# A four-layer graph kernel on one core: the first aggregation moves ahead of the heads, the head projections and the next graph's openings move behind them, and x rotates through three buffers

## The reference

```
x = LN(x + softmax((x Wq' + bq) (x Wk')' / sqrt(128)) (x Wv' + bv))        # attention over all nodes, mask of ones
x = LN(x + leaky(0.01, ((adj / rowsum(adj)) x) W1' + b1))                  # first aggregation
x = LN(x + heads(x, adj))        # 4 heads: e = leaky(0.2, si + sj), masked by adj, softmax over i, times Wh
x = LN(x + (D^-1/2 (adj + I) D^-1/2 x) B)                                  # second aggregation, D from adj + I
```

## Time and profile before

| | |
|---|---|
| Median of 3 timed executions | 977.44 us (975.45 to 979.87) |
| The profiled execution | 977.33 us, of which the span of instructions is 975.5 us |
| Granted TensorE clock, mean | 0.957 of full speed |
| Busy share of the span: PE, DVE, ACT, POOL | 87%, 75%, 60%, 33% |
| Period of a full step (first score groups at 202.70 and 317.25) | 114.5 us |

### The profile page before, as it was taken

How to read it: one execution, slowest core, us unless ns; L and a number is a source line. 1 busy time by engine, 2 the same in 40 slices (tenths; PEclk the granted TensorE clock), 3 DMA queues, 4 the chain that set the end, 5 groups by cost and what they waited for, 6 DMA issues and landing times.

```text
span 975.5 us, 25298 instructions
## 1 busy us (share of the span) xinstructions
PE 848.5 (87%) x10856; PEld 683.6 (70%) x10856; DVE 731.0 (75%) x1635; ACT 587.1 (60%) x668; POOL 326.3 (33%) x335
## 2 busy tenths in 40 slices
PE   4988999798998989889998989989899899974874
PEld 2664699556985679746896569856697468962873
DVE  3438777788768787689777887687877798765965
ACT  1564675667665766656846666657665667545513
POOL 2022511633034520626007240355207161064404
PEclk8998999999999999999999999999999999996897
DMA  9823116911178123760268211781237601700260
GB/s 184 123 65 70 41 46 89 164 54 44 50 105 153 45 87 53 121 134 2 87 90 151 66 44 46 97 164 46 76 59 130 111 20 67 89 2 23 67 89 22
DMA packets 166463, 77.39 MB, mean 79 GB/s; under 512 B 136624, under 2 KB 154160, under 8 KB 166352
## 3 DMA queue, kind: packets, MB, share of 16 engines
q1 hardware_dynamic: 156864, 58.48, 31.5%
q0 software_dynamic: 8448, 16.78, 9.7%
q10 hardware_dynamic: 1040, 0.52, 0.2%
HBM read 54.66 MB, written 4.33 MB: 60 GB/s over the span
## 4 chain that ended last, share of the span: by engine, by line
PE 36%; issue 25%; DVE 22%; POOL 7%; ACT 7%; DVEq 0%; POOLq 0%; ACTq 0%
PE ring L1200 7%; PE Z L1222 7%; PE ring L1254 5%; PE Z L1271 4%; DVE x L846 4%; DVE cmat L810 4%; DVE ring L755 3%; PE ring L1235 2%; ACT steps L654 2%; POOL rstd L471 2%; ACT maskb L591 2%; PE ring L1198 2%; DVE meanvar L839 2%; PE ring L1165 1%; DVE x L830 1%
## 5 line engine op out<-in xcount | busy, mean ns | idle before, releaser
L654 ACT ACTIVATE steps<-sjrow,steepsi 128x1024 bf16<-128x1024 f32 x248 | 267.5, 1139 | 123.3 <-DVE cmat L810 94.9
L810 DVE TENSOR_TENSOR cmat<-steps,adj 128x1024 f16<-128x1024 bf16 x180 | 153.6, 896 | 24.6 <-ACT steps L654 22.6
L1254 PE MATMUL ring<-vparts,cmat 128*128 128x66 bf16 x4416 | 146.2, 195 | 16.9 <-DVE cmat L810 12.1
L1222 PEld LDWEIGHTS Z<-vv,probs 128*128 128x128 f32 x1024 | 122.6, 191 | 52.6 <-ACT probs L661 37.3
L1254 PEld LDWEIGHTS ring<-vparts,cmat 128*128 128x128 f16 x4416 | 143.5, 98 | 18.4 <-issue 7.4
L1222 PE MATMUL Z<-vv,probs 128*128 128x129 f32 x1024 | 126.5, 277 | 25.4 <-ACT probs L661 25.4
L1200 PE MATMUL ring<-qT,xT 128*128 128x512 f32 x256 | 139.4, 627 | 0.0
L526 POOL TENSOR_TENSOR cmat<-cmat,ident 128x1024 f16<-128x1024 f16 x8 | 17.1, 2144 | 254.1 <-DMA cmat<-adj 254.1
L755 DVE CUSTOM_DVE_ANT_0 ring<-ring,maskb 128x1024 f32<-128x1024 f32 x64 | 78.3, 1227 | 29.0 <-PE ring L1138 16.3
L661 ACT ACTIVATE probs<-ring 128x1024 f32<-128x1024 f32 x64 | 65.0, 1015 | 52.1 <-PE ring L1200 52.1
L1235 PE MATMUL ring<-vparts,adj 128*128 128x132 bf16 x1536 | 94.0, 222 | 0.0
(11 more groups left out here) (126 smaller groups left out, 1376.3 us busy)
## 6 DMA issues: line engine op xcount, KB each, us to landing
adj<-in_adj_dram POOLq DMA_DIRECT2D x16, 1024.0 KB, 13.0
sjrow<-sj_rows SPq DMA_DIRECT2D x31, 512.0 KB, 4.1
out_dram<-x SPq DMA_DIRECT2D x16, 256.0 KB, 2.4
x<-in_x_dram SPq DMA_DIRECT2D x7, 512.0 KB, 4.3
adjT<-adj SPq DMA_TRANSPOSE x64, 3.5
cmat<-adj SPq DMA_TRANSPOSE x64, 4.5
x<-in_x_dram ACTq DMA_DIRECT2D x1, 512.0 KB, 4.4
small<-in_a_dram SPq DMA_DIRECT2D x1, 128.0 KB, 11.0
```

The source lines that it names most:

```text
L654: act.activation(steps[:, n % STEPS, :], sjrow[:, h % 2, :], ACT.Relu, bias=steepsi[:, t, h:h + 1], scale=STEEP).then_inc(step_made, 1)
L810: dve.tensor_tensor(c_of[:, t, :], steps[:, n % STEPS, :], adjs[o.parity][:, t, :], ALU.min)\
L1222: last = pe.matmul(zq[:, q, 0:D + 1], probs[:, n % 2, j, q * P:(q + 1) * P], vv[:, kt, :], start=kt == 0 and q % 2 == 0, stop=kt == T - 1, ...
L1254: last = pe.matmul(s[:, jt, 0:VW], c_of[:, t, jt * P:(jt + 1) * P], vparts[:, t, h, part, :], start=t == 0 and part == 0, stop=t == T - 1 ...
```

## The change

The list `ORDER` per kind of step becomes one list `SEQ` over all steps, made by `groups_of`. In a full step the first aggregation runs directly behind the mask sums and ahead of head 0, `out1` behind head 0, then heads 1 to 3. Behind head 3 stand the head projections of graph n (`x2T`, `wh`, `sj`) and, between them, the next graph's `xT`, `q` and `v`; then the second aggregation, and `s0` of the next graph between `out3` 0 and 1. The next step begins with `s1`. So the head projections of a graph move from the step after it into its own step, in the first step too, and the last step has none.

With it: `wide` has only four tiles in place of eight and each is used twice in an aggregation; both transposed adjacencies go through the one `adjT`; x rotates through three buffers, in place; `sj` goes through two of the `steps` buffers; ACT makes 14 in place of 17 comparison tiles between the exponentials (`PACE`) and `spread_largest` comes after the second score group; POOL's roots for layer 2 and the degrees come ahead of the diagonal, and the last step fetches all four `sj` rows by DMA.

```diff
+        masks, c = [("mask", 0), ("mask", 1)], [("c", h) for h in range(H)]
+        if n < NB:
+            seq += of(n - 1, *masks, c[0])
+        else:
+            seq += of(n - 1, c[0], *masks)
+        seq += of(n, ("out1", 0), ("out1", 1))
+        seq += of(n - 1, *c[1:])
+        if n < NB:
+            seq += of(n, ("x2T", 0)) + of(n + 1, ("xT", 0)) + of(n, ("wh", 0), ("wh", 1)) + of(n + 1, ("q", 0)) \
+                + of(n, ("sj", 0)) + of(n + 1, ("v", 0))
+        seq += of(n - 1, ("out3", 0))
+        if n > 0:
+            seq += of(n + 1, ("s", 0))
+        return seq + of(n - 1, ("out3", 1))
...
-    PACE = [0, 2, 2, 3, 3, 2, 2, 3]
+    PACE = [0, 2, 2, 2, 2, 2, 2, 2]
...
+        def wide_used_by(agg, g, t):
 
             n = max(0, 2 * g.base - 1) if agg == "agg1" else min(2 * g.base + 2, 2 * NB - 1)
-            return (T - 1) * (n - 1) + t + 1
+            return (T - 1) * n + t - 3 if t >= T // 2 else (T - 1) * (n - 1) + t + 5
...
 
-                if g.base > 0:
-                    sp.wait_ge(widened["agg1"], g.count(T))
+                if g.base == 1:
+                    sp.wait_ge(widened["agg1"], T)
+                elif g.base > 1:
+                    sp.wait_ge(widened["agg3"], g.before(2).count(T, T))
                 for t in range(T):
                     if t % 4 == 0:
                         sp.wait_ge(adj_in[g.parity][t // 4], g.count_own(16, 16))
                     sp.dma_start_transpose(adjT[:, :, t * P:(t + 1) * P], adjs[g.parity][:, t, :]).then_inc(turned, 16)
 
-            def turn_older(o):
-
-                sp.wait_ge(full["c"], o.count(2 * H, 4))
+            def turn_older(kind, o):
+
+                if kind == "last":
+                    sp.wait_ge(widened["agg3"], o.count(T))
+                else:
+                    sp.wait_ge(widened["agg1"], o.count(T, 2 * T))
                 for t in range(T):
-                    sp.dma_start_transpose(adjT_of_older[:, :, t * P:(t + 1) * P], adjs[o.parity][:, t, :])\
-                        .then_inc(turned_older, 16)
+                    sp.dma_start_transpose(adjT[:, :, t * P:(t + 1) * P], adjs[o.parity][:, t, :]).then_inc(turned_older, 16)
...
+                    degree_of(g)
+                    for k in range(2):
+                        rstd_of(1, g, [k])
                 if kind != "first":
                     add_diagonal(o)
-                    rstd_of(2, o)
                     if o.base < NB - 2:
 
                         pool.wait_ge(full["mask"], o.count(2, 2))
                         pool.wait_ge(c_made, o.count(H * T, H * T))
                         load_adj(Graph(o.base + 2))
-                if kind != "last":
-                    degree_of(g)
-                if kind != "first":
+                    rstd_of(2, o)
                     for k in range(2):
                         pool.wait_ge(split3, o.count(6, 3 * k + 1))
-                        norm_apply(2, o, x3, k)
-                if kind != "last":
-                    for k in range(2):
-                        rstd_of(1, g, [k])
+                        norm_apply(2, o, x_of(o), k)
 
             program(step)
...
+                    if kind == "first":
+                        make_maskb(Graph(1), range(4, T))
+                    else:
+                        made = steps_until(20)
+                    widen(g, "agg1", range(4, T))
                     take_sums("agg1", g, agg1T)
-                    make_maskb(Graph(1), range(4, T))
-                    return
-                for n in range(made, len(STEP_TILES[kind])):
-                    step_tile(kind, o, n)
-                if kind == "full":
-                    widen(kind, g, "agg1", range(T))
-                    take_sums("agg1", g, agg1T, [0])
-                    widen(kind, o, "agg3", [0])
-                    take_sums("agg1", g, agg1T, [1])
-                    widen(kind, o, "agg3", range(1, T))
-                else:
-                    widen(kind, o, "agg3", range(T))
-                take_sums("agg3", o, agg3T)
+                if kind != "first":
+                    made = steps_until(len(STEP_TILES[kind]))
+                    widen(o, "agg3", range(0, 4))
+                if kind != "last":
+                    following = Graph(g.base + 1)
+                    for name, graph, k in (("x2T", g, 0), ("xT", following, 0), ("wh", g, 0), ("wh", g, 1),
+                                           ("q", following, 0), ("sj", g, 0), ("v", following, 0)):
+                        if graph.base < NB:
+                            take_group(kind, graph if name != "sj" else g, name, k)
+                if kind != "first":
+                    widen(o, "agg3", range(4, T))
+                    take_sums("agg3", o, agg3T)
                 if kind == "full" and g.base < NB - 1:
                     make_maskb(Graph(g.base + 1), range(0, 4))
...
                 split_x1(g, 0)
                 context(g, 1)
-                norm_stats(0, g, x1, 1)
+                norm_stats(0, g, x_of(g), 1)
                 if kind == "full":
+                    mins(kind, o, 1, range(4, T))
                     sums_of_masks(kind, o, 0)
-                    mins(kind, o, 2)
-                    sums_of_masks(kind, o, 1)
-                norm_apply(0, g, x1, 1)
+                norm_apply(0, g, x_of(g), 1)
                 split_x1(g, 1)
                 if kind == "full":
+                    mins(kind, o, 2, range(0, 4))
+                    sums_of_masks(kind, o, 1)
+                    mins(kind, o, 2, range(4, T))
                     combine(kind, o, 0)
-                    mins(kind, o, 3)
-                    last_heads(kind, o)
                 for k in range(2):
                     layer1_out(kind, g, k)
-                    norm_stats(1, g, x2, k)
-                final = g.base == NB - 1
-                if kind == "full" and not final:
-
-                    layer3_out(kind, o, 0)
-                    layer3_out(kind, o, 1)
-                norm_apply(1, g, x2, 0)
-                norm_apply(1, g, x2, 1)
-                if final:
+                    norm_stats(1, g, x_of(g), k)
+                if kind == "full":
+                    mins(kind, o, 3, range(0, 4))
+                    combine(kind, o, 1)
+                    mins(kind, o, 3, range(4, T))
+                norm_apply(1, g, x_of(g), 0)
+                norm_apply(1, g, x_of(g), 1)
+                if kind == "full":
+                    combine(kind, o, 2)
+                    end_of_heads(kind, o)
+                    split_x3(o, 0)
+                    split_x3(o, 1)
+                largest_si(g)
+                if g.base < NB - 1:
+                    cast_x(Graph(g.base + 1))
+                    cast_q(Graph(g.base + 1))
+                if kind == "full":
                     layer3_out(kind, o, 0)
                     layer3_out(kind, o, 1)
...
+                    if g.base < 2:
+                        guard_scores(kind, g, 0)
+                    for t in range(1, 5):
+                        guard_scores(kind, g, t)
                     for n in range(T):
                         scores(kind, g, n)
                         if kind == "full" and n == 0:
-                            turn_largest(kind, g.before())
-                        if between_scores[n]:
-                            group(kind, g, *between_scores[n])
-                        if kind == "full" and n == 0:
-                            spread_largest(kind, g.before())
+                            turn_largest(kind, o)
+                        if n < 3:
+                            guard_scores(kind, g, 5 + n)
+                        if kind == "full" and n == 1:
+                            spread_largest(kind, o)
                         if n >= 1:
                             context(kind, g, n - 1)
                     context(kind, g, T - 1)
-                if kind == "last":
-                    turn_largest(kind, g.before())
-                    spread_largest(kind, g.before())
-                if kind == "first":
-                    pe.wait_ge(late_in, 48)
-                else:
-                    for name, k in ORDER[kind]:
-                        if name == "mask":
-                            mask_sums(kind, g, k)
-                        elif name == "c":
-                            head_sums(kind, g, k)
+                    if kind == "full":
+                        mask_sums(kind, g, 0)
+                        mask_sums(kind, g, 1)
+                    layer1(kind, g)
+                    if kind == "full":
+                        head_sums(kind, g, 0)
+                    finish_layer1(kind, g)
+                if kind != "first":
+                    for h in range(1, H):
+                        head_sums(kind, g, h)
                 if kind != "last":
-                    layer1(kind, g)
-                if kind == "first":
-                    finish_layer1(kind, g)
-                    pe.wait_ge(dve_init, 5)
```

(12 more changed lines are left out.)

393 lines of the change are left out of this document (188 added, 205 removed).

## The result

The changed kernel takes 1006.2 us (median of 4 runs, 1003.9 to 1007.2) against 977.1 us: a ratio of 1.029, 95% interval 1.026 to 1.032. It is slower; the forecast was 984, with slower at 0.53, and the time lies 4 us outside the range. The profiled execution has a span of 1002.0 us, 26.5 more than before. It is the fastest of the four executions, 2.3 us under their median, so what follows adds up to 26.5 us and not to the 29.1 between the medians.

A forecast was written before the change was run, and what follows sets the result against it. PE was taken to bound the step, with about 11 us of holes and 1.4 us of cold clock. Terms 2.5 (five steps at +0.5) + 2.4 + 10.6 - 4.6 - 4.7 + 0.3 = +6.5 on 977.3: 984 us, range 966 to 1002.

The forecast's parts named there:

- the clock's term: Cold PE clock after the hole before `st0`: 1.4 us a step, between 0 and 2.2.
- Scores: Score stage: last context ends 37.9 us after the start of `st0`, net -2.3 us a step.
- Head 3: Head 3 waits for VectorE's comparisons; `c3` ends 29.4 us after the first aggregation's end, +3.6 us.
- rival C: Small holes in `c3` and before `wh` 0 also cost the clock: 1.6 in six steps, 994 us; chance 0.12.
- Moved opening: Opening between head 3 and second aggregation: done 39.7 us after the first aggregation's end, +8.7 us a step.
- To the next `st0`: After the second aggregation with `out3` 0: 9.75 us to the next `st0`, -9.7 us a step.
- Step 1: Step 1 has no layer-4 norm and gains only 0.5 in the score stage: +2.4 us.
- Rival B: VectorE's chain from first aggregation's end to second's parts bounds the second half: 999 us; chance 0.16.
- Rival A: Score stage takes only PE's busy time, 35.6 us, if the clock survives the hole: 970 us; chance 0.22.
- D: Rival: head 3's gate does not appear, the bound does not move: -1.8 us a step, 973 us; chance 0.08.
- The end: Last two steps: -4.6 us from moved projections, -4.7 from the final aggregation's shorter wait, 0.3 back for clock.
- The first step: `x2T` now ahead of the second graph's opening: its `st0` at 102.4 instead of 91.78, +10.6 us.

The follow-up runs named there:

- e7: e2 plus ten idle matmuls in head 3's sums, ahead of the fifth tile: 985.2 us, ratio to before 1.007.
- e10: e6 plus the ten idle matmuls in head 3's wait, as in e7: 973.4 us, ratio to before 0.995.
- e6: Changed kernel with `sj` and `v` moved into the next opening's wait, second aggregation's sums copied to `small`: 974.9 us, ratio to before 0.997.
- e9: e6 plus the edit of e1, head 3's comparisons made earlier: 974.5 us, ratio to before 0.996.
- e2: Changed kernel plus idle matmuls (6 and 14) among the guard scores of each opening from the third graph on: 996.4 us, ratio to before 1.016.
- e5: Changed kernel with the second graph's `xT`, `q` and `v` done in the first step's wait for layer-1 output: 1005.8 us, ratio to before 1.029.
- e11: e10 with the first step's order of e5 and 28 idle matmuls in the wait left there: 973.6 us, ratio to before 0.995.
- e1: Changed kernel with head 3's comparisons made ahead of the two halves of the layer-1 output: 1002.0 us, ratio to before 1.021.
- e12: Kernel before the change plus 12 idle matmuls between `xT` and `q` in every opening but the first: 987.1 us, ratio to before 1.008.

## Why the prediction missed

The step that failed is the clock's term. In head 3 it was put at nothing: "`c3` ends at 24.1 + 7/8 of 6.0 = E+29.4" counts the work behind the new wait at full clock, 5.3 us, and it took 6.83. At `st0` it was sized too small: 1.4 us, measured 1.7 to 2.8. By the steps of the prediction, for a steady step:

- **Scores, R+37.9 forecast.** R+38.8 and +39.8 to +39.9 in turn. Without the clock's loss e7 gives R+37.1, where the layout gave 36.5: the order of exponentials and comparisons was right to 0.6 us. "The clock takes 1.4 back" was 1.7 or 2.7 to 2.8. I had sized it by the hole of 2.5 us at `q`; this hole is 3.57, behind another of 1.99.
- **Head 3, E+29.4.** E+31.2. The gate was right: last comparison at E+24.5 (24.1 forecast). The 7/8 of the head behind it is what took 6.83. That is rival C, given 0.12, and it is true for head 3 though not for `wh` 0. With the clock held the head ends at E+30.0.
- **Moved opening, E+39.7.** E+40.8; in e7 E+39.75.
- **To the next `st0`, 9.75 us.** 9.85.
- **Step 1, +2.4.** +5.3. In e7 this step takes 114.14 us instead of 116.19, and the excess over the forecast is 2.9. Of the 2.0 between the two, half is head 3, which e7 fills; the other half is the score stage, where e7 fills nothing ahead and the clock came back sooner all the same.
- **Rival B** (VectorE's chain) is not what bounds this kernel, e7 shows that; it bounds e10, and e6 and e9 to within half a microsecond. **Rival A**'s clock surviving the hole was what e2 made by hand, and it then gave R+37.1, not 35.6. **D** is out: the waits appear.

So +0.5 a step became +3.5: about 1.4 in the score stage, 1.8 in head 3 less 0.7 that the opening behind it won back, and some 0.5 in small terms. Over the program the clock is 21 us (1006.2 to 985.2). That 985.2 is one microsecond from the forecast is luck. The forecast had 1.4 us of low clock in each of six steps; without them, as e7 runs, it would have said some 976 (an estimate: 984 less 8.4). The ten microseconds between lie elsewhere: about 4 in the five steady steps, 1 in step 1, 3 at the end and 3 in the first step of e7's profile.

**The end, -9.0 forecast, -7.0.** The largest si was spread 4.4 us earlier (-4.6 forecast; but the prediction took 111.2 for a distance that is 111.9 by the start of 774.53, so its R+106.6 was 1.0 too early), and the final aggregation waited 5.13 instead of 10.67 (-4.7 forecast, -5.3 from head 1 on). What I had not laid out lies between them, 42.3 us instead of 38.8: head 1 now waits 5.61 us for VectorE, where it waited 1.97. Why VectorE is later there is open: this is read from the trace alone, and no run tests it.

```profile
957.90 7.78 PE L1267 MATMUL ring<-vparts,cmat 128*128 128x66 bf16 x192 [5.61 <-DVE small L910]
...
982.83 8.60 PE L1282 MATMUL Z<-wide,parts 128*128 128x512 f32 x30 [5.13 <-DVE parts L870]
```

**The first step**, +10.6 forecast, +10.8 measured. The agreement to 0.2 us is partly luck: the eight other kernels with the same first step have `st0` 0.5 to 2.8 us later than this profile. The reasons given are not shown by a run, since doing `xT`, `q` and `v` ahead brought back next to nothing in e5, and 2.3 us with the clock held in e11.

The rule that I weighed, on VectorE and GpSimd shutting each other out, was worth about a microsecond either way and did not decide. The diagonal fell on one instruction of `combine` 1, which took 1.68 us where its like take 0.42: 1.26 us lost, 1.1 forecast from the row, up to 2.14 by the rule. The trace bears the rule out. The two instructions before it, which have one input in PSUM (`ring`), took 0.42 each beside the same GpSimd operation; this one has both inputs in SBUF, and it ended 0.3 us behind GpSimd. What it lost was short of 2.14 because GpSimd had begun 1.0 us before it.

```profile
413.70 1.68 DVE L912 TENSOR_TENSOR small<-small,ex 128x264 f32<-128x264 f32 x1
412.73 2.36 POOL L546 TENSOR_TENSOR adjT<-adjT,ident 128x1024 f16<-128x1024 f16 x1
```

The comparisons' end at E+24.5 lies between the two sums (24.1, and 25.1 by the rule), and in e5 four single-input norm instructions lost 2.0 us beside a GpSimd addition of 2.34. The Trainium skill, "TensorE: Matmul & The Clock Gate", section "Part 1: The HAM clock gate (the "warmup" mystery)", puts the cost of warming up at under 1% of a typical kernel's span. Here it is more, 21 us of 1006, 2.1%, at two places that recur each step, and the measurement decides.

## What to carry to other kernels

A wait on PE can have two prices: its length, and the slow start of the work behind it. Allow for the second at every new wait of a few microseconds, as a range and not as one number. Count short bursts between small waits (three of 0.27 us here) as part of the hole; this last is read from one place, and no run tests the bursts alone. When a block is moved away from a wait that it covered, move the pieces that have no consumer nearby (here `v` and `sj`) into the wait that opens; that gave 31 us, and idle matmuls alone gave 21. And before filling a wait, find in the code every semaphore that PE waits for there: the profile names the last one, and filler placed behind an earlier one that is nearly as late is only work.

## What the runs showed of the hardware

- Idle matmuls hold the granted clock as well as useful ones: 20 short ones in the opening took the score stage from 0.96 to 1.00 (e2, e7), as `sj` and `v` there did for its first pairs (1.08 us each in e6), and ten in head 3 took its stretch from 0.95 to 1.00 (e7).
- The cost of one and the same wait varies from step to step without a change in the code: the score stage of the changed kernel alternates between 38.8 and 39.9 us, `wh` behind 3.74 us takes from 2.12 to 3.72 (e1), and behind 2.19 us the clock was 1.00 in one opening and 0.50 in the next (e12). Head 3's 171 matmuls take 6.7 to 7.0 us in the changed kernel and 7.5 in e2 and e6.
- Four VectorE instructions with one SBUF tensor operand took 3.12 instead of 1.12 us beside a GpSimd addition of 2.34 (e5).
